# ScalarE's silus, tanh and copies in another order, and four tap products over 66 rows made into three

## What is computed

```python
conv = conv_b + sum(x_pad[:, k:k + L, :] * conv_w[k, 0] for k in range(2))
proj = conv @ Wp + bp                                  # 64 + 64 columns
B_t, C_t = softplus(proj[..., :64]), tanh(proj[..., 64:])
y0 = C_t * scan(decay * state + dt * B_t * (x @ Ws + bs))   # a recurrence over 2048 steps
h = y0 @ Wo + bo                                       # 512 wide
x_br, z = split(layernorm(h) @ W_in)                   # 1024 + 1024
xb = silu(causal_conv4(x_br))                          # four taps for each channel
Bm, Cm, delta = xb @ W_b, xb @ W_c, softplus(xb @ W_delta + b_delta)
s_t = exp(delta * A) * s_(t-1) + delta * Bm * xb       # 1024 channels x 16 states
y = sum over states(s_t * Cm) + xb * Dp
x = x + (y * silu(z)) @ W_out + h
```

## Time and profile before

| what | value |
|---|---|
| median of 3 executions | 2659.27 us (2657.55 to 2660.13) |
| the profiled execution | 2653.91 us, its span 2651.9 us |
| instructions | 34212 |
| TensorE busy | 2309.5 us, 87% of the span |
| VectorE busy | 2265.5 us, 85% |
| GpSimd busy | 1728.4 us, 65% |
| ScalarE busy | 1669.0 us, 63% |
| granted TensorE clock, mean | 0.95 of full |

### The profile page before, as it was taken

One profiled execution on the slowest core, in us unless ns is written; L12 is line 12 of the kernel. 1 busy time (PEld: TensorE's weight loads), 2 busy tenths in 40 slices (PEclk: granted clock), 3 DMA queues, 4 the chain that ended last, 5 costly groups with the idle time before them and its releaser, 6 DMA issues. The chain is left out here.

```text
span 2651.9 us, 34212 instructions
## 1 busy us (share of the span) xinstructions
PE 2309.5 (87%) x11520; PEld 1586.2 (60%) x11520; DVE 2265.5 (85%) x2232; ACT 1669.0 (63%) x3332; POOL 1728.4 (65%) x2042
## 2 busy tenths in 40 slices
PE   7778889888898988888988888888888875999997
PEld 5566667676666666757666666666666322444443
DVE  2399999999999999899999999999999835888886
ACT  2567676667667676767676767676766534555554
POOL 0278787878787878778787778787878711222221
PEclk8889999999999999999999999999998987999999
DMA  4102020202010110102020202020104621111110
GB/s 186 72 1 72 9 76 6 76 5 80 16 65 21 61 53 28 65 17 73 9 72 10 72 10 72 10 76 5 72 10 189 233 83 56 60 64 66 59 52 24
DMA packets 48299, 151.74 MB, mean 57 GB/s; under 512 B 8069, under 2 KB 8965, under 8 KB 45198
## 3 DMA queue, kind: packets, MB, share of 16 engines
q1 hardware_dynamic: 48142, 149.76, 15.9%
HBM read 132.37 MB, written 17.37 MB: 56 GB/s over the span
## 5 line engine op out<-in xcount | busy, mean ns | idle before, releaser
L472 POOL TENSOR_TENSOR ring<-ring,Cbc 128x512 f32<-128x512 f32 x1024 | 1283.1, 1275 | 44.5 <-POOL carry L465 0.4
L864 DVE TENSOR_TENSOR_SCAN ring<-a_ps,ring 128x1024 f32<-128x1024 f32 x512 | 1168.0, 2281 | 106.7 <-ACT a_ps L702 105.2
L702 ACT ACTIVATE a_ps<-delta,nA 128x255 f32<-128x255 f32 x2048 | 852.9, 468 | 380.3 <-DVE ring L864 379.4
L1069 PE MATMUL yT_ps<-ident,ring 128*128 128x128 f32 x4096 | 588.1, 284 | 163.5 <-POOL ring L472 160.0
L1069 PEld LDWEIGHTS yT_ps<-ident,ring 128*128 128x128 f32 x4096 | 475.0, 145 | 282.2 <-POOL ring L472 241.9
L856 DVE TENSOR_TENSOR ring<-u_ps,Bbc 128x1024 f32<-128x1024 f32 x512 | 619.7, 1210 | 16.0 <-PE yT_ps L1069 9.3
L1035 PE MATMUL work<-xb,big 128*128 128x256 f32 x2048 | 476.8, 385 | 10.1 <-ACT zs L560 10.1
L1035 PEld LDWEIGHTS work<-xb,big 128*128 128x128 f32 x2048 | 385.5, 193 | 79.5 <-issue 16.9
L465 POOL TENSOR_TENSOR carry<-ring,half 128x4 f32<-128x4 f32 x512 | 127.1, 248 | 361.2 <-DVE ring L864 359.7
L1051 PE MATMUL work<-Wout,xb 128*128 128x512 f32 x512 | 237.7, 599 | 0.0
L1414 POOL TENSOR_TENSOR m<-m,pows 128x1 f32<-128x1 f32 x64 | 34.2, 549 | 311.4 <-DVE m L1546 311.4
(11 more groups left out here) (197 smaller groups left out, 2508.1 us busy)
## 6 DMA issues: line engine op xcount, KB each, us to landing
Bbc<-bc_rows SPq DMA_DIRECT2D x64, 512.0 KB, 4.6
Cbc<-bc_rows SPq DMA_DIRECT2D x64, 512.0 KB, 3.7
xT<-in_xT SPq DMA_DIRECT2D x16, 514.0 KB, 3.5
x_rows<-x2row SPq DMA_DIRECT2D x32, 256.0 KB, 2.0
xp<-x_rows SPq DMA_DIRECT2D x32, 256.0 KB, 2.7
xx<-in_x SPq DMA_DIRECT2D x32, 256.0 KB, 3.0
out_rows<-orow SPq DMA_DIRECT2D x32, 256.0 KB, 2.0
delta<-in_c_w SPq DMA_DIRECT2D x6, 1024.0 KB, 5.3
```

The source lines that it names most:

```text
L472: nc.gpsimd.tensor_tensor(hp, hp, Cbc[:, G * g + GP * c:G * g + GP * c + GP, :], ALU.mult)\
L702: r = nc.scalar.activation(a_ps[q % 2][:, i, 1:T], delta[:, par, dt, 1:T], ACT.Exp, scale=nA[:, dt, s:s + 1])
L864: dve.tensor_tensor_scan(ring[:, q % RING, :, :].rearrange("p g t -> p (g t)"), a_ps[q % 2][:, :, :].rearrange("p g t -> p (g t)"), ring[: ...
L1069: r = pe.matmul(yT_ps[:, tt, :], ring[:, q % RING, i, P * tt:P * tt + P], ident[:, :], is_transpose=True, start=False, stop=(g == NG - 1 a ...
```

## The change

ScalarE's tanh of the first projection and the two silus on z go together into a `visit` in slot 5, between two table loads; the silus on z are those of block k, gated in the same step, instead of those of block k + 1 in slot 30. `prj` and `prj_ln` move to slots 4 and 5, ahead of the visit, `gates0` to slot 3. The silus on x are split: the first half follows xcopy(1) in slot 15, the second xcopy(3) in slot 17, each with a table load on either side. `zcopy(2)` and `dexp(1)` move from slot 27 to 26, `dln(0)` from 28 to 27. The copy of y0 goes from VectorE to ScalarE. x's products: taps 0 and 1 share one product over 128 rows, with `yp` holding y0s's 64 rows twice, shifted by one; the two constant rows of these taps sit at rows 96 and 97 of the products of taps 2 and 3. `y0back` writes these copies. The diff, with unchanged lines cut:

```diff
@@ -31,6 +31,7 @@
...
 NY = N0 + 2
+CROW = 96
 EPS = 1e-5
...
@@ -117,7 +118,8 @@
...
-        Mx = big[0][:, 0:4 * DI].rearrange("p (k c) -> p k c", k=4)
+        Mx = big[0][:, 0:3 * DI].rearrange("p (k c) -> p k c", k=3)
+        yp = big[0][:, 3 * DI:3 * DI + T]
         Mz = big[0][:, 4 * DI:5 * DI]
...
@@ -154,8 +156,8 @@
...
         WoTg = xdp[:, :, :].rearrange("p a b -> p (a b)")[:, 0:KD * NY].rearrange("p (d n) -> p d n", d=KD)
-        MTk = ring[:, 1:RING, :, :].rearrange("p a b c -> p (a b c)")[:, 0:ND * 4 * NY]\
-            .rearrange("p (m k n) -> p m k n", m=ND, k=4)
+        MTk = ring[:, 1:RING, :, :].rearrange("p a b c -> p (a b c)")[:, 0:ND * 3 * P]\
+            .rearrange("p (m k n) -> p m k n", m=ND, k=3)
         cond = V[:, V_COND:V_COND + 2 * KD].rearrange("p (d b) -> p d b", b=2)
...
@@ -192,6 +194,7 @@
...
         s_mxs = sem("s_mxs")
+        s_mtz = sem("s_mtz")
         s_mxp = sem("s_mxp")
...
@@ -497,15 +500,29 @@
...
                         act.wait_ge(s_setD, 8)
+                    wait(act, s_c0, 6 * n)
                     nc.scalar.activation(e0[:, :], ps[0:N0, 0:T], ACT.Exp, bias=sc0[0:N0, 4:5]).then_inc(s_e0, 1)
-                    wait(act, s_c0, 6 * n)
-                    nc.scalar.activation(c0[:, :], ps[N0:P, 0:T], ACT.Tanh, bias=sc0[N0:P, 4:5]).then_inc(s_tanh, 1)
-
                 def prj_ln():
-                    nc.scalar.preload_act_table_set("natural_log_exp_and_others")
                     act.wait_ge(s_c0, 6 * n + 1)
                     nc.scalar.activation(e0[:, :], e0[:, :], ACT.Ln, bias=1.0).then_inc(s_l0, 1)
+
+                def visit():
+
+                    nc.scalar.preload_act_table_set("silu_and_others")
+                    if front:
+                        nc.scalar.activation(c0[:, :], work[BANK["PRJ"]][N0:P, 0:T], ACT.Tanh, bias=sc0[N0:P, 4:5])\
+                            .then_inc(s_tanh, 1)
+                    if scan:
+                        zsilu(k, par)
+                    nc.scalar.preload_act_table_set("natural_log_exp_and_others")
+
+                def keep_y0():
+
+                    if back:
+                        act.wait_ge(full[BANK["WOUT1"]], jobs_before("WOUT1", k) + 1)
+                    act.wait_ge(s_c0, 6 * n + 5)
+                    nc.scalar.activation(y0k[:, fp, :], y0[:, :], ACT.Copy).then_inc(s_c0, 1)
...
@@ -536,8 +553,14 @@
...
                     nc.scalar.activation(y0s[0:NY, fp, 0:3], y0s[0:NY, fp, T:T + 3], ACT.Copy).then_inc(s_yh, 1)
-                    act.wait_ge(s_yh, n + 1)
-                    nc.scalar.activation(y0s[0:NY, fp, 3:T + 3], ps[0:NY, 0:T], ACT.Copy).then_inc(free[BANK["YB"]], 1)
+                    act.wait_ge(s_yh, 2 * n + 1)
+                    nc.scalar.activation(y0s[0:NY, fp, 3:T + 3], ps[0:NY, 0:T], ACT.Copy).then_inc(s_yh, 1)
+                    act.wait_ge(s_yh, 2 * n + 2)
+
+                    nc.scalar.activation(yp[0:N0, :], y0s[0:N0, fp, 0:T], ACT.Copy)
+                    nc.scalar.activation(yp[N0:2 * N0, :], y0s[0:N0, fp, 1:T + 1], ACT.Copy)
+                    nc.scalar.activation(y0s[CROW:CROW + 2, fp, 2:T + 3], y0s[N0:NY, fp, 0:T + 1], ACT.Copy)\
+                        .then_inc(free[BANK["YB"]], 1)
...
@@ -548,8 +571,8 @@
...
                         act.wait_ge(s_mxp, m + 1)
-                        nc.scalar.activation(Mx[0:NY, :, P * m:P * m + P],
-                                             abank[2 + m % 2][0:NY, :].rearrange("p (k c) -> p k c", k=4), ACT.Copy)\
+                        nc.scalar.activation(Mx[:, :, P * m:P * m + P],
+                                             abank[2 + m % 2][:, 0:3 * P].rearrange("p (k c) -> p k c", k=3), ACT.Copy)\
                             .then_inc(s_mxc, 1)
...
@@ -568,12 +591,11 @@
...
-                def silu():
-                    for j in (ND // 2 - 2, ND // 2 - 1):
+                def silu(i):
+                    for j in (2 * i, 2 * i + 1):
                         act.wait_ge(free[BANK[f"XB{j}"]], jobs_before(f"XB{j}", k) + 1)
-                    for i in range(2):
-                        v = xb[:, fp, 4 * i:4 * i + 4, :].rearrange("p a b -> p (a b)")
-                        nc.scalar.activation(v, v, ACT.Silu).then_inc(s_xb, 1)
+                    v = xb[:, fp, 4 * i:4 * i + 4, :].rearrange("p a b -> p (a b)")
+                    nc.scalar.activation(v, v, ACT.Silu).then_inc(s_xb, 1)
                     nc.scalar.preload_act_table_set("natural_log_exp_and_others")
...
@@ -644,20 +666,19 @@
...
-                next_plan = {5: [prj], 6: [prj_ln], 8: [lambda: stats(0)], 9: [lambda: stats(1)], 10: [y0scale],
-                             11: [y0back], 14: [lambda: xcopy(0)], 15: [lambda: xcopy(1)], 16: [lambda: xcopy(2)],
-                             17: [lambda: xcopy(3), silu], 20: [bc], 21: [lambda: zcopy(0)], 23: [lambda: zcopy(1)],
-                             25: [lambda: dexp(0, False)], 27: [lambda: zcopy(2), lambda: dexp(1, False), lambda: dtail(0, False)],
-                             28: [lambda: zcopy(3), lambda: dln(0, False)], 30: [lambda: zsilu(n, fp)],
+                next_plan = {4: [prj], 5: [prj_ln], 8: [lambda: stats(0)], 9: [lambda: stats(1)], 10: [y0scale],
+                             11: [y0back], 13: [keep_y0], 14: [lambda: xcopy(0)], 15: [lambda: xcopy(1), lambda: silu(0)],
+                             16: [lambda: xcopy(2)], 17: [lambda: xcopy(3), lambda: silu(1)], 20: [bc],
+                             21: [lambda: zcopy(0)], 23: [lambda: zcopy(1)], 25: [lambda: dexp(0, False)],
+                             26: [lambda: zcopy(2), lambda: dexp(1, False)],
+                             27: [lambda: dtail(0, False), lambda: dln(0, False)], 28: [lambda: zcopy(3)],
                              31: [lambda: dexp(2, False)]}
...
-                    next_plan.update({27: [lambda: dexp(1, False), lambda: dtail(0, False)],
-                                      28: [lambda: dln(0, False), lambda: zcopy(2), lambda: zcopy(3)], 30: [], 31: []})
+                    next_plan.update({26: [lambda: dexp(1, False)], 28: [lambda: zcopy(2), lambda: zcopy(3)], 31: []})
                 scan_plan = {2: [lambda: dexp(3, True), lambda: dtail(1, True)], 6: [lambda: dln(1, True)]}
...
                     scan_plan[1] = [lambda: dexp(2, True)]
-                    scan_plan[3] = [lambda: zsilu(k, par)]
                 turned = {13: 0, 20: 1, 28: 2}
...
@@ -676,6 +697,8 @@
...
                         job()
+                    if q == 5 and (front or scan):
+                        visit()
                     if scan and q in turned:
...
@@ -721,6 +744,7 @@
...
             dve.tensor_scalar(nA[:, :, :], nA[:, :, :], -1.0, None, ALU.mult).then_inc(s_setD, 1)
+            dve.memset(MTk[:, :, 1:3, NY:P], 0.0).then_inc(s_mtz, 1)
             dve.wait_ge(s_w[0], 16)
...
@@ -771,21 +795,17 @@
...
-                def keep_y0():
-
-                    if back:
-                        dve.wait_ge(full[BANK["WOUT1"]], jobs_before("WOUT1", k) + 1)
-                    dve.wait_ge(s_c0, 6 * n + 5)
-                    dve.tensor_copy(y0k[:, fp, :], y0[:, :]).then_inc(s_c0, 1)
-
                 def mx_scale():
+                    dve.wait_ge(s_mtz, 1)
                     for m in range(ND):
...
                         ps = abank[m // 4][:, NY * (m % 4):NY * (m % 4) + NY]
-                        for tap in range(4):
-                            r = dve.tensor_scalar(MTk[:, m, tap, :], ps, V[:, V_CW + 4 * m + tap:V_CW + 4 * m + tap + 1],
-                                                  None, ALU.mult)
+                        cw = [V[:, V_CW + 4 * m + tap:V_CW + 4 * m + tap + 1] for tap in range(4)]
+                        for tap in range(2):
+                            dve.tensor_scalar(MTk[:, m, 0, N0 * tap:N0 * tap + N0], ps[:, 0:N0], cw[tap], None, ALU.mult)
+                            dve.tensor_scalar(MTk[:, m, 1 + tap, CROW:CROW + 2], ps[:, N0:NY], cw[tap], None, ALU.mult)
+                            r = dve.tensor_scalar(MTk[:, m, 1 + tap, 0:NY], ps, cw[2 + tap], None, ALU.mult)
                         r.then_inc(s_mxs, 1)
...
@@ -866,7 +886,7 @@
...
-                next_plan = {4: [gates0], 5: [scan0], 13: [keep_y0]}
+                next_plan = {3: [gates0], 5: [scan0]}
                 for q in range(NQ):
...
@@ -993,8 +1013,8 @@
...
                             pe.wait_ge(s_mxc, m - 1)
-                        for tap in range(4):
-                            r = pe.transpose(abank[2 + m % 2][0:NY, P * tap:P * tap + P], MTk[:, m, tap, :], ident[:, :])
+                        for i in range(3):
+                            r = pe.transpose(abank[2 + m % 2][:, P * i:P * i + P], MTk[:, m, i, :], ident[:, :])
                         r.then_inc(s_mxp, 1)
...
@@ -1004,16 +1024,15 @@
...
                     c = P * (2 * j + m)
-                    for tap in range(4):
```

(6 more changed lines are left out.)

## The result

| | kernel before | changed kernel |
|---|---|---|
| median | 2659.42 us (2657.55 to 2660.13, 4 runs) | 2688.26 us (2685.94 to 2690.30, 4 runs) |
| ratio | 1 | 1.0109 [1.0092, 1.0127] |
| the profiled execution; its span | 2653.91; 2651.9 us | 2685.94; 2683.9 us |
| granted TensorE clock, mean | 0.95 | 0.927 |

The change costs 29 us. The forecast was 2683 (2646 to 2710), slower, by the mechanism it gave for the steady blocks. Of the two profiled spans (one execution each), which differ by 32.0 us: up to the first scan -7.0, block 0 +0.1, blocks 1 to 14 +32.9, the last block +7.0, behind it -1.0 (from the start of each block's first scan in the two traces).

A forecast was written before the change was run, and what follows sets the result against it. VectorE was taken to bound the kernel, its scans waiting for ScalarE. (a), (b), (c) gave +2.3 us a block, +32 over 14; block 0 -3.4, ahead of the scans -5, last block +0.5: +24, 2683 us (2646 to 2710).

The forecast's parts named there:

- (a): Slots 3 to 9: the visit delays gT(3), stalling W_out and keeping the clock low; +2.4 us a block, +0.7 to +4.0.
- the clock's part: Around W_out in slot 4: work lost to the low TensorE clock behind the stall, 1.7 us, between nothing and 3.4.
- The wait ahead of slot 9's scan: Sign to look for: VectorE's wait for the transposes at slot 9 grows from 0.35 to 2 to 5 us.
- The rival in which the delay is absorbed: Slot 4: W_out's chain has 2 us more slack, (a) would be -0.9; -1.0 a block, 2637 us; chance 0.14.
- (b): Slots 10 to 17: fewer x products and split silus halve slot 17's wait of 3.6 us; -2.1 us a block.
- (c): Slots 23 to 31 and u: zcopy(2), dexp(1) a slot earlier make slot 26's scan wait 3.6 us; +2.0 a block.
- the better of the two cases: After the last scan, u slips in before GpSimd's second half: (c) +1.5 us, against +2.7 if it waits.
- Block 0: First block: no gT(3), so (a) is -0.6, and slot 3's wait of 2.68 us goes; -3.4 us.
- Ahead of the scans: Before the first scan: TensorE's 4.40 us wait for the silus and 3.5 us of products go, less copies and memset; about -5 us.
- The last block: Final block: visit without Ln and tanh, hidden to 0.1 us, and TensorE 0.7 late; +0.5 us.
- The rival of the spread low clock: Slots 27 to 29: low clock reaches delta's products, another 1.5 to 2 us a block, +50, 2709 us; chance 0.13.
- The rival of four more switches: ScalarE's table loads: four more switches, each holding it 1.3 us more than the row shows; over +80 us; chance 0.02.

The follow-up runs named there:

- joined silus with the same taps: Changed kernel with both silus on x joined in slot 17 again, as before the change: 2682.18 us, 1.0088 of the kernel before.
- gated y ahead: Changed kernel with ScalarE's gT(3) copy of the gated y moved to slot 5, ahead of Ln and the visit: 2656.39 us, 0.9986 of the kernel before.
- zcopy(2) in 27: Changed kernel with zcopy(2) and dexp(1) back in slot 27 and dln(0) in 28: 2656.26 us, 0.9984 of the kernel before.
- both: Changed kernel with gT(3) first in slot 5 and zcopy(2), dexp(1) back in slot 27: 2608.00 us, 0.9802 of the kernel before.
- four taps: Changed kernel with x's four tap products and without the three copies, ScalarE's new order kept: 2703.33 us, 1.0171 of the kernel before.
- silus joined: Changed kernel with both silus on x together in slot 17, as before the change: 2682.18 us, 1.0088 of the kernel before.
- load ahead: Changed kernel with gT(3) first in slot 5, zcopy(2), dexp(1) in 27, x silus joined, their table load before xcopy(3): 2576.55 us, 0.9693 of the kernel before.
- gated y between: Load ahead version with the gated y copy put behind the visit but ahead of slot 5's decay factors: 2594.98 us, 0.9762 of the kernel before.
- the taps alone: Kernel before with only the taps' part (three x products, their copies), ScalarE's order and y0's copy as before: 2618.06 us, 0.9843 of the kernel before.

## Why the prediction was right, and where it was off

The mechanism of the steady blocks was right, with one path wrong in (a). The ends of the kernel were not: they were put at -7.9 us together and came to -0.9. Three misses there (+3.5 in block 0, -2.0 ahead of the scans, +6.5 in the last block) cancel in part, and the medians differ by 29 us where the profiled spans differ by 32: that the whole fell only 5 us from the forecast owes something to luck. The profiled execution came 8 us above its 2678.

**(a) Slots 3 to 9, +2.4: right, measured +2.95** (-0.71 to slot 5, +2.47 to slot 7, +1.19 to slot 11). The stall of W_out was put at 2.0 us and is 1.80; the clock's part at 1.7, and the rows show 1.7 us lost in W_out's first six matmuls (2.05 and 2.62 against 1.07 and 1.88 at the full clock; 2.6 in the next block), of which the kernel before lost 0.5 in W_out's first product. On average over blocks 1 to 14 the six take 1.42 us more than before, where the forecast had 1.7 - 0.5 = 1.2. What I had wrong is the place. I looked for slack at slot 9, found none and charged the delay there; the chain bites first at slot 7, where VectorE waits for slot 4's turned states, which stand behind W_out in TensorE's order. There the slack was some 2.4 us (the turn ended at 1146.96, VectorE wanted it at 1149.4), and the delay of 4.04 us (1.14 of it clock) used it up. The wait ahead of slot 9's scan, which was to grow from 0.35 to 2 to 5 us, stands at 0.83; the prediction's own sign speaks against the path that it gave for (a). The rival in which the delay is absorbed would have needed 4 us of slack.

**(b) Slots 10 to 17, -2.1: right, measured -2.22**; slot 17 waits 1.43 where I had 1.6. (Its times for x(1)'s copy, loads and silu add up to 1178.25, not 1178.45, too little to matter.) The remark that the split brings two loads was right and too mild: joined silus with the same taps do it in 0.4 less. The 3.5 us of TensorE's products give -2.61 by themselves, more than the whole of (b); the split silus, -0.95 beside four products, take 0.4 of it away beside three.

**(c) Slots 23 to 31 and u, +2.0: right, measured +2.59 and -0.87, so +1.7.** The wait at 26 is 3.3 for 3.6, with ScalarE's 6.45 for "6"; 3.5 us of TensorE's time saved in slot 14 to 17 bring z(2) no earlier, as said. The u product slipped in, the better of the two cases. (The prediction had it end with GpSimd's pair in the kernel before; by its rows the pair ends at 1245.03 and u at 1245.59, so most of u's own 0.67 us lies behind the pair.)

**Per block** +2.35 for +2.3, 14 of them +32.9 for +32. Period 127.4 to 129.0 us.

**Block 0, -3.4: wrong, measured +0.1.** The wait of 2.68 in slot 3 went, but slots 0 to 5 fell by 0.35 us only. I had counted what goes and not what is late next. VectorE, block 0, after:

```profile
104.92 2.29 DVE L884 TENSOR_TENSOR_SCAN ring<-a_ps,ring 128x1024 f32<-128x1024 f32 x1 [5.59 <-ACT a_ps L725]
...
115.61 1.29 DVE L774 TENSOR_SCALAR e<-e 64x256 f32<-64x256 f32 x1 [0.54 <-ACT e L504]
```

Slot 1's wait grew from 4.59 to 5.59, and the small recurrence, moved to slot 3, waits 0.54 there and takes 1.29. And its slots 23 to 31 took 3.4 us more instead of 2.4.

**Ahead of the scans, -5: measured -7.0, part of it chance.** TensorE's wait for the silus did not go, as I had it; it fell from 4.40 to

```profile
65.36 3.61 PE L1043 MATMUL work<-xb,Wbc 128*32 128x256 f32 x16 [3.58 <-ACT xb L598]
```

and the sixteen products behind it took 3.61 us instead of 6.42: the granted clock over them was 1.00, before 0.56. That is not the change's doing. The version with the gated y ahead differs only from step 1 on, and there the same sixteen products, behind the same wait of 3.58, took 6.41 us and the first scan began 3.6 us later. By it and the two beside it (zcopy(2) in 27, both) the change gives 3.5 to 4.3 us here.

**The last block, +0.5: wrong, measured +7.0**, the worst term. Its W_out, where TensorE waits 0.58 us for the late copy, and the turns behind it, after and before:

```profile
2049.87 2.05 PE L1068 MATMUL work<-Wo,big 128*128 128x512 f32 x2 [0.58 <-ACT xb L648]
2051.71 5.31 PE L1070 MATMUL work<-Wout,xb 128*128 128x512 f32 x10
...
2067.99 3.65 PE L1088 MATMUL yT_ps<-ident,ring 128*128 128x128 f32 x16
```

```profile
2023.19 1.60 PE L1049 MATMUL work<-Wo,big 128*128 128x512 f32 x2
2024.62 4.46 PE L1051 MATMUL work<-Wout,xb 128*128 128x512 f32 x10
...
2039.61 1.94 PE L1069 MATMUL yT_ps<-ident,ring 128*128 128x128 f32 x16
```

Of the 7.0, 5.4 lie in slots 7 to 11. The granted clock over the sixteen turns was 0.50, before 1.00. I had given the clock to the steady blocks and not to this one. It is not the order of ScalarE as such: over the twelve kernels the last block took 124.1 to 131.1 us, 130.2 in the kernel with the load ahead and 124.3 in the same kernel with the gated y between; where the low stretches fall seems to set it, but each kernel has one profiled last block, and no run holds the rest still.

**The rival of the spread low clock** (chance 0.13) had a true core. Delta's products of slot 27 do begin low in the changed kernel (2.7 to 3.6 us for the eight, 1.99 at the full clock), and slots 23 to 31 take 31.8 to 32.2 us where blocks with products at the full clock take 31.7 (every second block of the kernel with four taps, and of the one with the silus joined, TensorE idle for the same 3.29 us ahead of them): 0.1 to 0.5 us. With the copy of the gated y ahead every block has the eight wholly low and slots 23 to 31 take 33.12, so 1.4 us more, near the rival's 1.5 to 2; with four taps every second block has, at 32.9. So it was partly luck that the changed kernel paid so little for it.

**The rival of four more switches** had their number wrong: a block has six table loads after the change and five before, so one more. At 1.29 us from load to next instruction in every run, its longer price did not show either.

## What to carry to other kernels

Ask of each moved job what it stands in front of, not only what it stands behind: both costs here were a cheap copy (0.60 us) or a ready set of decay factors put behind something that waits, and moving the two back turned +1.1% into -2%, of which the taps alone give -1.6%. A table load belongs in front of the operation that waits for another engine, if that operation runs under both sets. Whether work is worth splitting between two visits to a table set hangs on what else bounds the stretch: here the split gained 0.95 us a block beside four products and lost 0.4 beside three. Follow a delay on a shared in-order queue to the first reader of every job behind it: the nearest wait shown is not the nearest deadline.
